# Fewer VectorE operations in a router's turn, and an output projection that collects bias and residual in a PSUM bank of its own

## The reference

```python
x = x + xattn(layernorm(x), ctx)          # 16 heads of 8; softmax over 64 context rows; out @ Wo + bo
h = layernorm(x)
scores = sigmoid(h @ gate_w.T) + gate_bias # 64 experts in 8 groups
# keep the 4 groups with the highest maximum, then the 6 best experts of what is left
topk_w = topk_w / (topk_w.sum(-1) + 1e-8)
routed = sum over the 6 of topk_w * (silu(h @ eg_w.T) * (h @ eu_w.T)) @ ed_w.T
x = x + shared(h) + routed                 # shared: one expert that every token passes
```

## Time and profile before

| | |
|---|---|
| median of three runs | 602.49 us (600.42 to 602.98) |
| the profiled execution | 603.01 us, its span 601.2 us |
| mean granted TensorE clock | 0.76 of 2.4 GHz |
| busy share of the span | PE 75%, DVE 74%, ACT 54%, POOL 67% |

### The profile page before, as it was taken

How to read it: one execution, slowest core, us unless ns; L and a number is a source line. 1 busy time by engine, 2 the same in 40 slices (tenths; PEclk the granted TensorE clock), 3 DMA queues, 4 the chain that set the end, 5 groups by cost and what they waited for, 6 DMA issues and landing times.

```text
span 601.2 us, 11457 instructions
## 1 busy us (share of the span) xinstructions
PE 450.1 (75%) x3212; PEld 369.3 (61%) x3212; DVE 443.1 (74%) x1803; ACT 325.1 (54%) x930; POOL 401.8 (67%) x426
## 2 busy tenths in 40 slices
PE   2688888787887887752699997999999999992000
PEld 1455555555655555431599996889988999982000
DVE  6546898899889889987564657788888758893222
ACT  2465454544445444221237994889888758991000
POOL 3000477777767667687777777777777777777773
PEclk9986565656557557555589996999999999997555
DMA  6812333333333333343456664667667788754221
GB/s 197 271 61 88 110 132 129 130 129 131 126 126 116 126 119 130 122 155 135 138 158 209 209 179 121 186 187 198 177 195 192 215 230 225 213 144 131 61 61 39
DMA packets 98703, 90.19 MB, mean 150 GB/s; under 512 B 10576, under 2 KB 85456, under 8 KB 98640
## 3 DMA queue, kind: packets, MB, share of 16 engines
q1 hardware_dynamic: 85232, 63.99, 34.2%
q0 software_dynamic: 12288, 25.19, 14.6%
q10 hardware_dynamic: 1120, 0.28, 0.2%
HBM read 41.19 MB, written 48.23 MB: 149 GB/s over the span
## 4 chain that ended last, share of the span: by engine, by line
PE 39%; DVE 17%; ACT 14%; POOL 12%; issue 11%; DMA 2%; ACTq 2%; DVEq 1%; POOLq 0%; SPq 0%
PE bank_s L1225 17%; PE bank_q L1225 7%; PE bank_o L1225 5%; POOL old_pages L475 4%; POOL empty L553 3%; ACT d_now L572 3%; PE bank_r L1225 3%; ACT gu_now L572 3%; DVE xb L1163 2%; POOL p_t L553 2%; ACT pxt L572 2%; PE bank_o L1326 2%; POOL new_pages L475 2%; PE bank_s L1221 2%; ACTq L572 2%
## 5 line engine op out<-in xcount | busy, mean ns | idle before, releaser
L475 POOL DMA_INDIRECT old_pages<-xn,place_i x144 | 150.6, 1046 | 67.0 <-issue 26.5
L1225 PE MATMUL bank_s<-pxt,gu_now 128*128 128x64 f32 x768 | 95.2, 278 | 4.5 <-ACT pxt L572 3.2
L1225 PEld LDWEIGHTS bank_s<-pxt,gu_now 128*128 128x128 f32 x768 | 91.1, 195 | 8.9 <-ACT pxt L572 8.9
L1177 DVE TENSOR_TENSOR h_t<-bank_s,s_act 64x256 f32<-64x256 f32 x128 | 54.5, 426 | 52.2 <-ACT s_act L725 49.7
L553 POOL DMA_INDIRECT empty<-old_results,place_i x72 | 68.6, 953 | 21.9 <-issue 19.2
L553 POOL DMA_INDIRECT p_t<-old_results,place_i x72 | 68.5, 952 | 21.9 <-issue 18.6
L475 POOL DMA_INDIRECT new_pages<-xn,place_i x48 | 47.3, 986 | 14.6 <-issue 13.4
L594 ACT ACTIVATE p_t<-bank_s 128x512 f32<-128x512 f32 x64 | 33.0, 603 | 39.4 <-PE bank_s L1225 39.4
L725 ACT ACTIVATE s_act<-bank_s 64x512 f32<-64x512 f32 x64 | 37.8, 590 | 30.3 <-PE bank_s L1225 25.2
L468 POOL TENSOR_TENSOR rstd<-ve,minus_half 128x4 f32<-128x4 f32 (+1 forms) x21 | 18.6, 886 | 50.2 <-DVE ve L988 46.1
L1163 DVE SCALAR_TENSOR_TENSOR xb<-empty,weight,xb 128x128 f32<-128x128 f32 x96 | 33.8, 352 | 22.9 <-DMA empty<-new_results,place_i 20.0
(11 more groups left out here) (177 smaller groups left out, 1055.2 us busy)
## 6 DMA issues: line engine op xcount, KB each, us to landing
pg<-old_pages SPq DMA_DIRECT2D x44, 256.0 KB
old_results<-y_s SPq DMA_DIRECT2D x44, 256.0 KB, 2.6
old_pages<-empty SPq DMA_DIRECT2D x14, 768.0 KB, 4.5
pg<-new_pages SPq DMA_DIRECT2D x20, 256.0 KB
new_results<-y_s SPq DMA_DIRECT2D x20, 256.0 KB, 2.8
new_pages<-empty SPq DMA_DIRECT2D x6, 768.0 KB, 4.6
w_gu<-in_expert_gu SPq DMA_DIRECT2D x16, 256.0 KB, 2.9
w_d<-in_expert_d SPq DMA_DIRECT2D x31, 128.0 KB, 3.1
```

Source lines behind the costliest of these rows:

```text
L475: pool.indirect_dma_start(out=(new_pages if n >= SPLIT else old_pages)[:, :], out_offset=bass.IndirectOffsetOnAxis(ap=place_i[:, TPB * n + ...
L1177: dve.tensor_tensor(h_t[q % 2][h * INTER:(h + 1) * INTER, :, h, :], gu_ps[q % 2][INTER:2 * INTER, :].rearrange("p (g h t) -> p g h t", g=Q ...
L1225: return pe.matmul(dst, w, v, start=True, stop=True)
```

## The change

In VectorE's part, per turn: the counts now come with `fill` already in them (`count_choosers` multiplies the bf16 `fill` in by three more products), so that `rank` and `filled_to` are views of `ranks`; the three comparisons that made `opens` become a multiplication and a rounding; the copy of `top_at` to bf16 is gone, and `is_expert` compares with the 32-bit integers themselves; the sum, its small addend, the reciprocal and the product that made `weight` are done once for all batches (`make_weights`), behind quad 3. The output projection moves to `bank_w`. There the bias product and two products of the residual with the identity come first (`residual`), ahead of `transpose_o`, and the projection adds to them. VectorE takes its statistics straight from `bank_w`, ScalarE copies the sum to `xb` (`keep_x2`), and `values` no longer waits for `x2_done`.

```diff
-ROUTE_STEPS = 18
-PLACE_STEPS = 19
+ROUTE_STEPS = 14
+PLACE_STEPS = 14
+FILL_STEP = 5
...
-        fill = sb("fill", [P, E])
+        fill = sb("fill", [P, E], BF16)
...
-        rank = sb("rank", [P, TPB, E])
-        filled_to = sb("filled_to", [P, E])
-        full = sb("full", [P, E])
+        rank, filled_to = ranks[:, 0:TPB, :], ranks[:, TPB, :]
+        opens_to = sb("opens_to", [P, E])
...
+            def keep_x2(b):
+
+                act.wait_ge(st2_done, TPB * (b + 1))
+                copy(xb[:, TPB * b:TPB * (b + 1), :], bank_w[:, 0:TPB * D].rearrange("p (t h) -> p t h", h=D)).then_inc(x2_done, 1)
+
...
                 if on(b + 2):
                     evacuate_v(b + 2)
+                if on(b - 1):
+                    keep_x2(b - 1)
                 if on(b + 3):
                     normalise_x(b + 3, side)
...
-                chained("sum", dve.tensor_reduce(wsum[:, :], top[:, :, 8 - TOPK:8], AX.X, ALU.add))
...
-                chained("divisor", dve.tensor_scalar(wsum[:, :], wsum[:, :], 1e-8, None, ALU.add))
...
-                chained("factor", dve.reciprocal(wsum[:, :], wsum[:, :]))
-                after("factor")
-                chained("weight", dve.tensor_tensor(weight[:, TPB * n:TPB * (n + 1), :], top[:, :, 8 - TOPK:8],
-                                                    wsum[:, :].unsqueeze(2).to_broadcast([P, TPB, TOPK]), ALU.mult))
...
-                chained("filled_to", dve.tensor_tensor(filled_to[:, :], ranks[:, TPB, :], fill[:, :], ALU.add))
-                chained("rank", dve.tensor_tensor(rank[:, :, :], ranks[:, 0:TPB, :], both(fill), ALU.add))
-                chained("expert", dve.tensor_copy(expert_h[:, :, :], top_at[:, :, 8 - TOPK:8]))
-                after("filled_to")
-                chained("full", dve.tensor_scalar(full[:, :], filled_to[:, :], float(U), None, ALU.is_gt))
...
+                chained("pages_to", dve.tensor_scalar(opens_to[:, :], filled_to, OPEN_SLOPE, -OPEN_SHIFT, ALU.mult, ALU.add))
...
-                more = full
-                for m in range(2, MOST_OPENED + 1):
-                    chained(("opens", m), dve.scalar_tensor_tensor(out=opens[:, :], in0=filled_to[:, :], scalar=float(m * U),
-                                                                   in1=more[:, :], op0=ALU.is_gt, op1=ALU.add))
-                    more = opens
-                    after(("opens", m))
+                after("pages_to")
+                chained("opens", dve.tensor_scalar(opens[:, :], opens_to[:, :], WHOLE, -WHOLE, ALU.add, ALU.add))
+                after("opens")
...
-                    experts(expert_h[:, :, :]), ALU.is_equal))
+                    experts(top_at[:, :, 8 - TOPK:8]), ALU.is_equal))
...
-            def add_attention(b):
-                dve.wait_ge(wo_done, b + 1)
-                xt = xb[:, bass.ds(TPB * b, TPB), :]
-                dve.tensor_tensor(xt, bank_o[:, TOK:2 * TOK].rearrange("p (t h) -> p t h", h=D), xt, ALU.add).then_inc(x2_done, 1)
-
             def residual_stats(n):
+                dve.wait_ge(wo_done, n + 1)
                 for t in range(TPB):
-                    stats(n, t, st2, st2_done)
+                    dve.bn_stats(st2[:, t, :], bank_w[:, t * D:(t + 1) * D]).then_inc(st2_done, 1)
...
             def count_choosers(n):
+                if n > 0:
+                    pe.wait_ge(placed, PLACE_STEPS * (n - 1) + FILL_STEP)
                 pe.wait_ge(chosen_ready, n + 1)
...
+                    pe.matmul(cols, row_h[0:VW, :], fill[0:VW, :], start=True, stop=False)
...
                 if b == 0:
                     pe.wait_ge(bias_part, BIAS_STEPS)
-                else:
-                    pe.wait_ge(x2_done, b)
...
+            def residual(b):
+
+                rows = slice(0, PARTS * VW)
+                if b > 0:
+                    pe.wait_ge(x2_done, b)
+                    pe.wait_ge(st2_done, TPB * b)
+                pe.matmul(bank_w[:, 0:TPB * D], row_h[rows, :], bias_h[rows, :], start=True, stop=False)
+                for t in range(TPB):
+                    pe.matmul(bank_w[:, t * D:(t + 1) * D], ident[:, :], xb[:, TPB * b + t, :], start=False, stop=False)
+
             def out_projection(b):
                 pe.wait_ge(ot_ready, b + 1)
-                rows = slice(0, PARTS * VW)
-                pe.matmul(bank_o[:, TOK:TOK + TPB * D], row_h[rows, :], bias_h[rows, :], start=True, stop=False)
                 for t in range(TPB):
-                    last = pe.matmul(bank_o[:, TOK + t * D:TOK + (t + 1) * D], o_t[:, t * P:(t + 1) * P], wo_s[:, :],
+                    last = pe.matmul(bank_w[:, t * D:(t + 1) * D], o_t[:, t * P:(t + 1) * P], wo_s[:, :],
                                      start=False, stop=t == TPB - 1)
                 last.then_inc(wo_done, 1)
```

More of the change, by code:

```diff
@@ L50 @@
 U = P // 2
-MOST_OPENED = TOK // U
+OPEN_SLOPE, OPEN_SHIFT, WHOLE = 0.01558, 0.499, 1.5 * 2 ** 23
+assert all(round(OPEN_SLOPE * f - OPEN_SHIFT) == max(f - 1, 0) // U for f in range(U + TOK + 1))
 HALVES = P // U
@@ L254, in build @@
         ranks_done, ranks_ready, placed = sem("ranks_done"), sem("ranks_ready"), sem("placed")
-        place_ready, digits_made, counted, codes_done, codes_ready = sem("place_ready"), sem("digits_made"), sem("counted"), sem("codes_done"), sem("codes_ready")
+        place_ready, digits_made, counted, weighed, codes_done, codes_ready = sem("place_ready"), sem("digits_made"), sem("counted"), sem("weighed"), sem("codes_done"), sem("codes_ready")
         scattered = [sem(f"scattered{i}") for i in range(XN2_SLOTS)]
@@ L898, in find_rows @@
-                after("filled_to")
-                chained("full", dve.tensor_scalar(full[:, :], filled_to[:, :], float(U), None, ALU.is_gt))
-                after("rank")
+                    dve.wait_ge(fresh, 1)
+                chained("pages_to", dve.tensor_scalar(opens_to[:, :], filled_to, OPEN_SLOPE, -OPEN_SHIFT, ALU.mult, ALU.add))
                 chained("row_here", dve.scalar_tensor_tensor(out=row[:, :, :], in0=rank[:, :, :], scalar=-float(U),
                                                              in1=both(base2), op0=ALU.add, op1=ALU.add))
-                after("full")
@@ L910, in find_rows @@
+                after("opens")
                 last_page = first_page[:, :] if n in (0, SPLIT) else next_page[:, n - 1, E - 1:E]
                 chained("pages", dve.tensor_tensor_scan(next_page[:, n, :], opens[:, :], zeros[:, :], last_page, ALU.add, ALU.add))
-                chained("fill", dve.scalar_tensor_tensor(out=fill[:, :], in0=opens[:, :], scalar=-float(U),
-                                                         in1=filled_to[:, :], op0=ALU.mult, op1=ALU.add))
+                if n == SPLIT - 1:
+                    chained("fill", dve.memset(fill[:, :], 0.0))
+                else:
+                    chained("fill", dve.scalar_tensor_tensor(out=fill[:, :], in0=opens[:, :], scalar=-float(U),
+                                                             in1=filled_to, op0=ALU.mult, op1=ALU.add))
@@ L914, in find_rows @@
+                assert places_at["fill"] == FILL_STEP
                 midway()
@@ L928, in find_rows @@
                                                            in1=both(jump), op0=ALU.is_ge, op1=ALU.mult))
-                chained("move", dve.tensor_tensor(move[:, :], jump[:, :], full[:, :], ALU.mult))
+                chained("move", dve.scalar_tensor_tensor(out=move[:, :], in0=opens[:, :], scalar=0.0, in1=jump[:, :],
+                                                         op0=ALU.is_gt, op1=ALU.mult))
                 after("jumped")
@@ L1108, in _, with make_weights @@
                 body(b)
+            def make_weights():
+                dve.tensor_reduce(wsum[:, :], top[:, :, 8 - TOPK:8], AX.X, ALU.add).then_inc(weighed, 1)
+                dve.wait_ge(weighed, 1)
+                dve.tensor_scalar(wsum[:, :], wsum[:, :], 1e-8, None, ALU.add).then_inc(weighed, 1)
+                dve.wait_ge(weighed, 2)
+                dve.reciprocal(wsum[:, :], wsum[:, :]).then_inc(weighed, 1)
+                dve.wait_ge(weighed, 3)
+                dve.tensor_tensor(weight[:, :, :], top[:, :, 8 - TOPK:8], wsum[:, :].unsqueeze(2).to_broadcast([P, B * TPB, TOPK]),
+                                  ALU.mult).then_inc(weighed, 1)
             def count_units():
@@ L1259, in count_choosers @@
             def count_choosers(n):
+                if n > 0:
+                    pe.wait_ge(placed, PLACE_STEPS * (n - 1) + FILL_STEP)
                 pe.wait_ge(chosen_ready, n + 1)
-                mm(bank_r[:, 0:E], before_h[:, :], chosen[:, 0, :])
-                pe.matmul(bank_r[:, E:2 * E], before_h[:, :], chosen[:, 1, :], start=True, stop=False)
-                pe.matmul(bank_r[:, E:2 * E], ones_h[:, :], chosen[:, 0, :], start=False, stop=True)
-                pe.matmul(bank_r[:, 2 * E:3 * E], ones_h[:, :], chosen[:, 0, :], start=True, stop=False)
```

(9 more changed lines are left out.)

21 lines of the change are left out of this document (9 added, 12 removed).

## The result

The changed kernel takes 586.5 us (median of 4 runs, 585.0 to 587.2) where the kernel before took 601.45 in the same session: ratio 0.9754, 95% interval 0.9723 to 0.9785, 2.5% faster. The forecast was 593.0 with a range of 588 to 600. The time lies under the range, where rival C stood: GpSimd has become the bound of the turns too.

A forecast was written before the change was run, and what follows sets the result against it. GpSimd's stream was fixed after 255.44 us, so only earlier turns could gain: 3.6 (clock as now) + 5.7 (three more fast turns) + 0.5 (first scatter), together 9.8, took 603.0 to 593.2; median put at 593.0, range 588 to 600.

The forecast's parts named there:

- rival C: GpSimd becomes the bound of the turns too, needing nearly every turn below 14.6 us: 587 to 589 us, chance 0.1.
- What bounds the kernel: GpSimd's stream after 255.44 us is fixed; faster turns before it come off the whole, at most 15.9 us of waits.
- The turn at 1.2 GHz: Turn with TensorE as the chain: -0.95 us before `q_less`, +0.85 for the residual, sum -0.1, between -0.5 and +0.5.
- The new wait for `xn`: TensorE's `transpose_x` waits for ScalarE's `xn`, behind `keep_x2` and two normalisations: 0.1 to 0.3 us a turn.
- The turn with a spell: Turn with a spell at 2.4 GHz, VectorE leading from 135.16 us: -0.6 us, a turn of 14.5.
- The clock: Three more turns see a spell at 2.4 GHz, 1.9 us each, 5.7 in all; mean clock near 0.68.
- My 9.3 (3.6 + 5.7): Gain over the turns: 3.6 us with the clock as now, 5.7 from three more turns at 2.4 GHz.
- The first scatter: GpSimd's first scatter, behind three turns at 2.4 GHz, comes some 0.5 us earlier.
- `is_expert` and the statistics: VectorE: `is_expert` loses no double rate by giving up bf16; each statistic from PSUM costs 0.05 us more, 0 to 0.13.
- D: ScalarE's chain is 0.5 us longer, `transpose_x` waits, the 1.2 GHz turn is 0.35 longer: 600 to 603 us, chance 0.08.
- B: TensorE's clock stays as it is, one turn in three with a spell: 597.5 to 600 us, chance 0.15.
- E: Slower: the new period misses the clock and no turn sees a spell: about 606 us, chance 0.07.

The follow-up runs named there:

- experiment 1: Kernel before with the projection part alone (residual, own bank, `keep_x2`, statistics from it): 600.1 us, ratio 0.9978.
- experiment 10: Changed kernel with two of twelve scatters left out in the first twelve batches, so GpSimd has less work: 570.5 us, turns of 13.81 us.
- experiment 7: Kernel before with the changes to ranks and pages alone (with the `fill` products), weights left in the turns: 593.05 us, ratio 0.9901.
- experiment 5: Kernel before, unchanged, run once more with a profile: 602.4 us, first scatter at 65.19 us.
- experiment 11: Kernel before with two of twelve scatters left out in the first twelve batches: turns of 15.85 us.
- experiment 3: Kernel before with 11 scatters in each turn's list of GpSimd in place of 10: 596.4 us, ratio 0.991.

## Why the prediction was wrong, point by point

**What bounds the kernel** was read rightly. From the last wait on GpSimd's stream is fixed, and the turns' gain comes off the whole, up to a floor. The floor set how much came off: GpSimd's idle time fell by 13.6 of the 15.9 that I had counted as waits, and I gave that case one chance in ten. (By its own terms the sum should also end at 592.7: 593.2 less the 0.5 by which the profiled execution lay above the median.)

**The turn at 1.2 GHz.** VectorE's list gives 0.48 of the 0.55 forecast, the weights nothing, as forecast. The residual's two products hold the next product back by 0.86 in the changed kernel's turn from 131.24 on, at 1.2 GHz (138.41 to 139.27 in the rows below); I took 0.85. From the start of the raw scores to the end of the projection that turn takes 5.39 us (from 136.20), a turn of before 4.43 (163.13 to 167.56). The sum of -0.1 can't be read by itself, since every ordinary turn of the changed kernel and of experiment 1 saw some of the full clock. The last one saw none in either kernel and went from 15.41 to 14.86; I had 0.5 for it.

```profile
138.41 1.06 PE L1333 MATMUL bank_w<-xb,ident 128*128 128x128 f32 x4
139.27 0.63 PE L1223 MATMUL bank_o<-ident,o_s 128*128 128x128 f32 x2
```

**The new wait for `xn`.** At `transpose_x` it was forecast at 0.1 to 0.3 a turn, behind `keep_x2` and the two normalisations. It is 0.8 (9.5 us in twelve turns), behind that same queue of ScalarE, but not at 1.2 GHz where I had weighed it. All eight waits lie in stretches at the full clock. There the stream of `values` takes TensorE 1.07 us (from 123.12) instead of 1.93, so that it comes to `transpose_x` early, and ScalarE's chain is no shorter. In the slow turn from 131.24 on there is none. I had not seen the other one, at the transposes of the second norm. The light changed kernel of experiment 10 shows whose it is, in the same view:

```profile
PE bank_q L1228 <- ACT xn L634: 11.2, 9, 1.9
PE bank_r L1228 <- ACT xn L634: 4.6, 10, 0.8
```

With less for GpSimd to do, `bank_r`'s falls from 12.1 to 4.6, and `bank_q`'s stays.

**The turn with a spell.** I had 14.5 for it. At the same clock the ranks part alone makes 14.49 (experiment 7), so the 0.9 for ranks was more like 0.6; the rest of that sum can't be read, since the changed kernel has no such turn that GpSimd leaves alone. The step that failed is the next one.

**The clock: "Each turn that changes sides gives 16.4 - 14.5 = 1.9", three of them.** I let turns pass from one kind of before to the other kind of before, with its one spell of 6.8 us. The changed kernel has turns of a third kind, at the full clock nearly from end to end, as the one of 12.97 us at 0.93 above. The changed kernel's shortest turn, and two stretches of it with a clock of 1.00 over 20 and over 17 us:

```profile
147.02:160.46 13.44, 10.23 (x87) 7.00 (x87) 12.77 (x54) 7.72 (x22) 10.49 (x12) 0.91 0.42 145
49.00:69.00 20.00, 15.09 (x149) 10.35 (x145) 16.93 (x72) 14.18 (x39) 5.97 (x6) 1.00 0.23 80
199.10:215.90 16.80, 12.93 (x121) 8.46 (x121) 15.19 (x55) 9.37 (x26) 13.16 (x13) 1.00 0.37 126
```

I had expected a mean clock near 0.68 from 62 to 240 us; it is 0.73 there, and 0.75 over the twelve turns, where it was 0.58. Freed of GpSimd (experiment 10, at a clock of 0.79) such turns are 13.8 us long on average, 2.0 shorter than before, or 24 us over twelve. My 9.3 (3.6 + 5.7) was two fifths of that. GpSimd's floor cut it to 13.6. Why the clock passes to that third kind no run shows; the runs show only which kernels have it.

The Trainium skill ("TensorE: Matmul & The Clock Gate", the part on the clock gate) has sustained activity release the clock. The runs agree in direction: 0.58 before, 0.65 with the VectorE part's shorter turns, 0.67 with the residual added and turns no shorter, 0.75 with both, 0.79 with the residual twice. The prediction's sentence that every spell of the kernel before follows on unbroken work was too wide: before the short one at 106.0 us TensorE had worked for 3.2 of 4.0 us.

**The first scatter**, forecast 0.5 earlier, came 4.9 earlier. As I treated it, it was a trifle. It is one only as long as GpSimd waits later on; once it hardly waits, each microsecond counts. Even so, experiment 5 shows part of the 4.9 to be chance.

**`is_expert` and the statistics.** `is_expert` takes 953 ns from the integers where it took 952, and a statistic from PSUM takes 289 ns, as from SBUF; my 0.05 for each wasn't needed. The 0.065 estimated from the Trainium skill ("VectorE: DVE Perf Modes", the section on the TRN2 errata) isn't seen either. For the double rate the same page of the skill (the section on what auto-detection checks) also asks for a step of one in every operand. The expert numbers are broadcast here, 64 times each, with a step of zero, so the skill's rule, read in full, gives no loss either. I had weighed the table without that condition. The changed kernel's groups, columns as in the earlier trace rows:

```profile
L912 DVE TENSOR_TENSOR is_expert<-iota_h,top_at 128x768 bf16<-128x768 bf16 x12 | 11.4, 953 | 0.0
L960 DVE BATCH_NORM_STATS2 st<-bank_w 128x6 f32<-128x128 f32 x24 | 5.9, 289 | 14.3 <-PE bank_w L1338 14.3
```

**The rivals.** C is what happened: the median lies 0.5 us below its range, the start gave 4.9 where it had 0.5, and its condition, nearly every turn below 14.6, wasn't met (seven of the twelve are longer; they average 14.71). D's wait is there and larger than I put it, but in turns with the full clock, where it takes up slack that TensorE has won. B and E fell with the clock.

## What to carry to other kernels

When several engines are within a few per cent of being the bound, the parts of a change don't add up: work taken from one side alone turned into longer waits for the others (experiments 1 and 7), both together gave more than the sum, and a third engine's own work cut that off. So work out for each engine what a turn would take if it never waited, and give the largest its due as the floor; GpSimd's could be read in the profile before: ten scatters of 1.05 us with 0.30 ahead of each and a power of 0.96 are 14.5 us a turn. And where a forecast moves cases between kinds already seen, ask whether a kind not yet seen can come up.

## What the runs showed of the hardware

A scatter's time on GpSimd depends on what VectorE does beside it. Beside most operations it takes 0.95 us. Beside the run from `is_expert` to `place_i` it takes up to 1.75 in the changed kernel: of its 192 scatters 30 take over 1.1 us, and 28 of these lie there. One such place, selected rows in order of time:

```profile
133.15 0.35 DVE L948 RECIPROCAL rsum<-bank_o 128x32 f32<-128x32 f32 x1
133.42 0.90 DVE L935 TENSOR_TENSOR picked<-is_expert,row 128x768 f32<-128x768 bf16 x1
133.69 1.45 POOL L475 DMA_INDIRECT old_pages<-xn,place_i  x1 [0.30 <-issue]
134.23 0.42 DVE L953 TENSOR_TENSOR o_s<-bank_o,rsum 128x256 f32<-128x256 f32 x1
134.56 0.95 DVE L942 TENSOR_REDUCE place_i<-picked 128x12 int32<-128x768 f32 x1
135.45 0.95 POOL L475 DMA_INDIRECT old_pages<-xn,place_i  x1 [0.30 <-issue]
```

The next one, which starts as `place_i` ends, is back at 0.95. Which of the operations does it was not tried. The Trainium skill ("GPSIMD Engine Reference", Specifications) says that GpSimd shares its interfaces to SBUF with VectorE and names operations with two inputs in SBUF as a source of contention. `picked` is one, and the trace agrees so far; `place_i`, with one input, lies beside the same scatters, and the rows don't separate the two. But `is_expert` has two inputs in SBUF as well, and the one scatter that lies almost wholly beside it takes 0.96 us in either kernel, so two inputs alone don't decide it. The 144 scatters of the old pages take 152.8 us where 144 x 0.95 would be 136.8, on the engine that sets the end; a scatter right behind a power, at 1.03, has a small share in it.

Executions of one kernel differ in the clock's spells from the start on. Four executions have the same code up to the first scatter. From 35 us to that scatter their mean clock is 0.70 (the profile of before), 0.84 (experiment 5), 0.88 (experiment 11) and 1.00 (experiment 3), and the scatter starts at 67.7, 65.2, 64.4 and 63.6 us, in the same order. That the clock is the whole of these 4 us was not tried by itself.
